# Layer normalisation of a graph-network pipeline moved between two engines, with the pipeline written out instead of looped

## The reference

```python
def _layernorm(x, axis=-1, eps=1e-05):
    m = jnp.mean(x, axis=axis, keepdims=True)
    v = jnp.var(x, axis=axis, keepdims=True)
    return (x - m) / jnp.sqrt(v + eps)

h = jnp.maximum(_layernorm(x, axis=-1), 0.0)
x = x + _L0_gnn_ref(h, adj, L0_gnn_W, L0_gnn_a)
h = jnp.maximum(_layernorm(x, axis=-1), 0.0)
x = x + _L1_gnn_ref(h, adj, L1_gnn_a0, L1_gnn_a1, L1_gnn_a2, L1_gnn_a3)
h = jnp.maximum(_layernorm(x, axis=-1), 0.0)
x = x + _L2_gnn_ref(h, L2_gnn_adj, adj, L2_gnn_weight, L2_gnn_bias)
h = jnp.maximum(_layernorm(x, axis=-1), 0.0)
x = x + _L3_gnn_ref(h, adj, L3_gnn_W, L3_gnn_a)
```

## Time and profile before

| | before |
|---|---|
| median of 3 runs | 351.57 us (351.4 to 351.6) |
| profiled execution, first to last instruction | 350.0 us |
| PE, DVE, ACT, POOL busy | 321.6, 312.2, 307.3, 252.4 us |
| instructions | 10115 |
| TensorE clock granted, mean | 0.993 |

### The profile page before, as it was taken

One profiled execution on the slowest core, in us unless ns is written; L12 is line 12 of the kernel. 1 busy time (PEld: TensorE's weight loads), 2 busy tenths in 40 slices (PEclk: granted clock), 3 DMA queues, 4 the chain that ended last, 5 costly groups with the idle time before them and its releaser, 6 DMA issues.

```text
span 350.0 us, 10115 instructions
## 1 busy us (share of the span) xinstructions
PE 321.6 (92%) x2568; PEld 293.3 (84%) x2568; DVE 312.2 (89%) x1603; ACT 307.3 (88%) x775; POOL 252.4 (72%) x396
## 2 busy tenths in 40 slices
PE   1899999999999997999999997999999999999981
PEld 0699899889989986979998986988998999988971
DVE  2889999989999969998999996998999999998864
ACT  1499889999999969999999986999999998999991
POOL 4866755898888644798988773589888875589632
PEclk9999999999999999999999999999999999999997
DMA  4900000550110000272101000057011000000011
GB/s 120 292 4 2 3 0 3 170 194 18 47 46 19 1 4 0 61 221 80 45 31 45 1 0 2 1 157 203 16 45 46 15 1 0 1 2 1 18 47 63
DMA packets 15976, 17.67 MB, mean 50 GB/s; under 512 B 2752, under 2 KB 11840, under 8 KB 15936
## 3 DMA queue, kind: packets, MB, share of 16 engines
q1 hardware_dynamic: 15936, 17.25, 16.3%
HBM read 13.05 MB, written 4.19 MB: 49 GB/s over the span
## 4 chain that ended last, share of the span: by engine, by line
PE 26%; issue 21%; POOL 21%; DVE 18%; ACT 9%; SPq 1%; DMA 1%; POOLq 1%; DVEq 0%; ACTq 0%
PE bank L844 6%; POOL rs L346 6%; POOL h L351 4%; DVE neg_s L595 4%; POOL xb L361 4%; PE bank L811 4%; ACT upper L450 3%; PE bank L778 3%; POOL h L354 3%; ACT prob L458 3%; PE bank L826 3%; DVE st L533 3%; POOL result L368 3%; PE bank L792 2%; PE bank L806 2%
## 5 line engine op out<-in xcount | busy, mean ns | idle before, releaser
L346 POOL TENSOR_TENSOR rs<-ve,minus_half 128x2 f32<-128x2 f32 x128 | 90.4, 706 | 62.6 <-DVE ve L552 61.5
L458 ACT ACTIVATE prob<-neg_s,neg_max 128x256 f32<-128x256 f32 x192 | 87.0, 502 | 10.9 <-DVE neg_max L595 10.4
L595 DVE CUSTOM_DVE_ANT_0 neg_s<-bank,upper 128x256 f32<-128x256 f32 x192 | 73.1, 416 | 9.2 <-ACT upper L450 6.9
L844 PE MATMUL bank<-val,pT 128*128 128x129 f32 x512 | 67.7, 275 | 0.0
L465 ACT ACTIVATE pT<-bank 128x512 f32<-128x512 f32 x96 | 57.7, 601 | 9.0 <-PE bank L826 8.0
L354 POOL TENSOR_TENSOR h<-h,rs 128x256 f32<-128x256 f32 x96 | 59.3, 617 | 7.5
L826 PE MATMUL bank<-ident,prob 128*128 128x128 f32 x384 | 58.0, 274 | 5.5 <-ACT prob L458 5.2
L844 PEld LDWEIGHTS bank<-val,pT 128*128 128x128 f32 x512 | 62.2, 191 | 0.2
L450 ACT ACTIVATE upper<-bank,val 128x256 f32<-128x256 f32 x128 | 52.6, 461 | 3.6 <-PE bank L815 3.4
L815 PE MATMUL bank<-absent,ident_bf 128*128 128x256 bf16 x192 | 52.8, 275 | 0.0
L811 PE MATMUL bank<-ident,val 128*128 128x128 f32 x256 | 47.2, 280 | 4.9 <-ACT val L441 3.6
(11 more groups left out here) (61 smaller groups left out, 656.2 us busy)
## 6 DMA issues: line engine op xcount, KB each, us to landing
edges<-in_adj SPq DMA_DIRECT2D x32, 256.0 KB, 3.0
xin<-in_x SPq DMA_DIRECT2D x32, 128.0 KB, 2.4
out_x<-result SPq DMA_DIRECT2D x32, 128.0 KB, 1.7
w_rel<-in_L_gnn_weight SPq DMA_DIRECT2D x1, 256.0 KB, 4.4
w_gat<-in_L_gnn_W SPq DMA_DIRECT2D x2, 64.0 KB, 2.0
a_gat<-in_L_gnn_a SPq DMA_DIRECT2D x4, 0.5 KB, 2.0
a_rel<-in_L_gnn_a SPq DMA_DIRECT2D x4, 0.5 KB, 3.5
bias<-in_L_gnn_bias SPq DMA_DIRECT2D x1, 64.0 KB, 4.7
```

The costliest lines, as they stand in the source:

```text
L346: pool.tensor_tensor(rs[:, k], ve[:, k], minus_half[:, :], ALU.pow).then_inc(rs_ready, 1)
L458: last = act.activation(prob[:, k % 4, t], neg_s[:, k % 4, t], ACT.Exp, bias=neg_max[:, k, t:t + 1], scale=-1.0)
L595: last = dve.tensor_tensor_reduce(out=neg_s[:, k % 4, t], in0=bank_z(k)[:, t], in1=upper[:, k % 4, t], scale=-1.0, scalar=3.0e38, op0=ALU. ...
L844: last = pe.matmul(bank_o(k)[:, t], pT[:, k % 4, u, t * P:(t + 1) * P], values[:, u], start=(u == 0), stop=(u == T - 1))
```

## The change

There are four edits.

1. The pipeline is written out. `pipeline(stages)` goes over all 128 units with constants; `eng.Fori` is gone, and so are the semaphore adds that stand beside SP's waits. The same stages run in the same order.
2. `center` goes from POOL to DVE. The two POOL operations of 128 x 256 become two DVE `tensor_scalar`, one a half of 128 x 128, which subtract the mean and multiply by the inverse deviation, both read from SBUF as a scalar for each partition. On DVE it stands at lag 1, for layers 0 and 3 behind `take_z`, for layer 1 just ahead of `rectify`. `less_mean` and its wait fall away.
3. `check_edges` is taken out on ACT. In its place the mask is computed as (adj - 1) * BIG on the adjacency read as unsigned, so that a value over 1 makes a score huge; the row maxima of layer 0 of all 32 graphs are kept (`neg_max0`), and at the end one comparison over 64 columns looks for such a value.
4. SP's load of the next adjacency waits for layer 0's mask and no longer for the check.

```diff
-    with eng.Fori(0, ROUNDS - 1) as rnd:
-        for s in range(PEELED, STEPS_A_ROUND):
-            step(s, rnd, rnd)
-        for s in range(PEELED):
-            step(s, rnd + 1, rnd)
+def pipeline(stages):
+    for s in range(len(ORDER) + LAG_MAX):
         for stage, lag, layers in stages:
+            if 0 <= s - lag < len(ORDER) and ORDER[s - lag][0] in layers:
+                stage(s - lag, *ORDER[s - lag])
...
-            def center(rnd, layer, k):
-                pool.wait_ge(rs_ready, nth(rnd, ALL, layer, k))
-                pool.tensor_tensor(h[:, k, :, 1:], (xin if layer == 0 else x1)[:, k],
-                                   mv[:, k, :, 0:1].to_broadcast([P, T, D]), ALU.subtract).then_inc(less_mean, 1)
-                pool.wait_ge(less_mean, nth(rnd, ATTEND, layer, k))
-                pool.tensor_tensor(h[:, k, :, 1:], h[:, k, :, 1:],
-                                   rs[:, k, :].rearrange("p (t o) -> p t o", o=1).to_broadcast([P, T, D]),
-                                   ALU.mult).then_inc(centered, 1)
...
-            def check_edges(rnd, layer, k):
-                act.wait_ge(edges_loaded[k], rnd * 16 + 16)
-                act.wait_ge(edges_checked, nth(rnd, RGCN_REL, 2, k))
-                act.activation(squares[:, :], edges[:, k].rearrange("p t n -> p (t n)"), ACT.Square,
-                               bias=minus_half[:, 0:1],
-                               accum_out=distances[:, bass.ds(rnd * SLOTS + k, 1)]).then_inc(edges_checked, 1)
...
+            def center(n, layer, g):
+                k = g % SLOTS
+                dve.wait_ge(rs_ready, nth(ALL, n))
+                for t in range(T):
+                    last = dve.tensor_scalar(h[:, k, t, 1:], (xin if layer == 0 else x1)[:, k, t],
+                                             mv[:, k, t, 0:1], rs[:, k, t:t + 1], ALU.subtract, ALU.mult)
+                last.then_inc(centered, 1)
...
-                                             edges[:, k, t].rearrange("p (q u) -> p u q", u=T),
-                                             0.0, -BIG, ALU.is_le, ALU.mult)
+                                             edges[:, k, t].bitcast(u32).rearrange("p (q u) -> p u q", u=T),
+                                             -1.0, BIG, ALU.add, ALU.mult)
...
-                           (invert_sums, 7, LAST), (mean_and_variance, 0, LAST), (residual, 7, FIRST),
+                           (center, 1, GATS), (invert_sums, 7, LAST), (mean_and_variance, 0, LAST), (residual, 7, FIRST),
...
-                           (residual, 7, MULTI_REL), (rectify, 1, MULTI_REL), (mean_and_variance, 0, FIRST)])
-            dve.wait_ge(edges_checked, B + 1)
-            dve.tensor_scalar(other[:, :], distances[:, :], T * N * 0.25 + 0.5, None, ALU.is_gt).then_inc(flag_step, 1)
+                           (residual, 7, MULTI_REL), (center, 1, MULTI_REL), (rectify, 1, MULTI_REL), (mean_and_variance, 0, FIRST)])
+            dve.wait_ge(z_taken, len(ORDER))
+            dve.tensor_scalar(other[:, :], neg_max0[:, :, :].rearrange("p b t -> p (b t)"), -0.5 * BIG, None,
+                              ALU.is_lt).then_inc(flag_step, 1)
```

More of the change, by code:

```diff
@@ L20, with nth @@
 ROUNDS = B // SLOTS
-STEPS_A_ROUND = 4 * SLOTS
 ALL, ATTEND, GATS, NORMED, MULTI_REL, RGCN_REL = (0, 1, 2, 3), (0, 1, 3), (0, 3), (1, 2), (1,), (2,)
 NOT_LAST, NOT_MULTI, FIRST, LAST = (0, 1, 2), (0, 2, 3), (0,), (3,)
+ORDER = [(layer, rnd * SLOTS + k) for rnd in range(ROUNDS) for layer in range(4) for k in range(SLOTS)]
+UNIT = {unit: n for n, unit in enumerate(ORDER)}
+COUNTS = {layers: list(itertools.accumulate(int(layer in layers) for layer, _ in ORDER))
+          for layers in (ALL, ATTEND, GATS, NORMED, MULTI_REL, RGCN_REL, NOT_LAST, NOT_MULTI, FIRST, LAST)}
 LAG_MAX = 9
[L27 to L48, removed]
-        for stage, lag, layers in stages:
[L50 to L53, removed]
-    for s in range(PEELED):
-        step(s, 0, None)
-    with eng.Fori(0, ROUNDS - 1) as rnd:
-        for s in range(PEELED, STEPS_A_ROUND):
-            step(s, rnd, rnd)
-        for s in range(PEELED):
-            step(s, rnd + 1, rnd)
[L62 to L65, removed]
+def nth(layers, n):
+    return COUNTS[layers][n]
+def pipeline(stages):
+    for s in range(len(ORDER) + LAG_MAX):
+        for stage, lag, layers in stages:
+            if 0 <= s - lag < len(ORDER) and ORDER[s - lag][0] in layers:
+                stage(s - lag, *ORDER[s - lag])
 GAT = ["stats", "aggr", "eps", "rstd", "norm", "xT", "hT", "wh", "v", "z", "relu", "e", "exp",
@@ L286, in store @@
[L286 to L291, removed]
-            for k in range(SLOTS):
[L295 to L307, removed]
@@ L426, in normalize, with take_hT @@
                 last.then_inc(h_ready, 1)
[L428 to L435, removed]
+            def take_hT(n, layer, g):
+                k = g % SLOTS
+                act.wait_ge(hT_put, nth(ATTEND, n))
+                act.activation(hT[:, n % 4], bank_x(n), ACT.Relu).then_inc(hT_ready, 1)
@@ L481, in _, with take_pT, elu_exponential @@
-            pipeline(act, [(take_v, 3, RGCN_REL), (elu_exponential, 8, LAST), (check_edges, 6, RGCN_REL),
+            def take_pT(n, layer, g):
+                k = g % SLOTS
+                act.wait_ge(pT_put, nth(ATTEND, n))
+                act.activation(pT[:, n % 4], bank_p(n), ACT.Copy).then_inc(pT_ready, 1)
+            def elu_exponential(n, layer, g):
+                k = g % SLOTS
+                act.wait_ge(o_taken, nth(ALL, n))
+                act.activation(expy[:, n % 4], y[:, n % 4], ACT.Exp).then_inc(expy_ready, 1)
@@ L639, in _, with elu @@
-            pipeline(dve, [(add_eps, 1, MULTI_REL), (elu_lower, 9, LAST), (statistics, 0, MULTI_REL),
+            def elu(n, layer, g):
+                k = g % SLOTS
+                dve.wait_ge(expm_ready, nth(LAST, UNIT[3, g]))
+                if g >= SLOTS:
+                    dve.wait_ge(stored[k], 16 * (g // SLOTS))
+                dve.tensor_tensor(result[:, k], expy[:, n % 4], y[:, n % 4], ALU.max).then_inc(elu_ready, 1)
+            pipeline([(add_eps, 1, MULTI_REL), (elu_lower, 9, LAST), (statistics, 0, MULTI_REL),
```

294 lines of the change are left out of this document (159 added, 135 removed).

## The result

The changed kernel takes 372.01 us (median, 371.44 to 372.28) against 351.49 for the kernel before on the same chip: the ratio is 1.0582, with a 95% interval of 1.0567 to 1.0597. It is 20.5 us slower. The forecast was 358 us with a range of 346 to 367, so the direction was right and the time is outside the range.

A forecast was written before the change was run, and what follows sets the result against it. PE, DVE and ACT were all near nine tenths busy; DVE and PE were the limits in octets 0 and 1. 350.0 - 5.1 (loop) + 12.2 (center) = 357.1 of span, plus 1.6 gives 358.7; forecast 358 us, range 346 to 367.

The forecast's parts named there:

- The loop: Pipeline written out: two DVE issue stalls at the loop's way back go, 2.76 less 0.21 us each, -5.1 us.
- The check and the loads: check_edges off ACT and earlier adjacency loads: worth nothing, since PE and DVE are as full and no row waits.
- DVE becomes the pace setter: With center on DVE, its round is 81.5 us against PE's 76, making DVE the most loaded engine.
- The price of a half: One 128-column center tensor_scalar on DVE costs 0.21 us in the queue, 0.42 a unit; outer bounds 0.137 and 0.30.
- Nothing waits for `center` on DVE: In DVE's queue center waits for its unit's power only at octet 3's start, some 0.1 us in two steps a round.
- Waits for POOL disappear: DVE's waits for POOL's center, 2.7 us a round in expy, mask and haT, vanish; nb's go on.
- Octet 3: Fourth eight-step stretch of a round: DVE replaces POOL as limit, 15.88 us becomes 16.7.
- The sum: A round of four octets is 23.9 + 23.6 + 19.6 + 16.7 = 83.8 us, +3.4; together +12.2 us.
- the dear one: Rival for center on DVE: a half costs 0.30 us, a round +6.4, time 370 us; chance 0.11.
- Free scalars: Rival for center on DVE: scalars cost nothing, 0.137 us a half, a round 79.6, time 344 us; chance 0.12.
- Relief counts: Rival: ACT and POOL relief counts, octets 22.9, 22.6, 19.0, 15.5, a round 80.0, time 345 us; chance 0.13.

The follow-up runs named there:

- experiment 2: The kernel before, only written out, with check_edges still on ACT, center on POOL and the 64-column comparison at the end; 345.78 us against 351.84.
- e1: The changed kernel with center back on POOL as two operations, all else as changed; 345.44 us against 351.84 for the kernel before.
- Experiment 6: The changed kernel with take_hT of layer 3 moved from DVE to ACT; 366.56 us, +15.3 over the kernel before. Its second run is e10.
- e5: The changed kernel with center's mean replaced by the constant 0.0, inverse deviation still read from SBUF; 362.93 us, +11.7 over the kernel before.
- experiment 5: The changed kernel with layer 1's center moved up DVE's list, ahead of the statistics' aggregation and away from rectify; 367.92 us, +16.1 over the kernel before.
- e3: The changed kernel with both scalars of center replaced by the constants 0.0 and 1.0; 354.66 us, +2.8 over the kernel before.
- e10: e1 (center on POOL) with take_hT of layer 3 moved from DVE to ACT; 347.60 us, -4.3 against the kernel before.
- e7: The changed kernel with center of layers 0 and 1 back on POOL, layer 3's on DVE; 354.21 us, +3.0 over the kernel before.
- e11: e1 with center of layer 1 alone on DVE, just ahead of rectify; 360.67 us, +8.3 over the kernel before.

## Why the prediction was wrong, step by step

Edit 2 was given +12.2 us and cost 26.9. Two steps of its sum failed: the price of a half was too low (0.21 us, measured 0.256), and `rectify`'s wait for `center` on DVE itself, about 4 us, was left out.

- *The loop (right).* -5.1 us was forecast, -6.1 measured in experiment 2. The next octet gave nothing back: 15.88 us before, 16.01 in e2. No wait of DVE for issue above 0.2 us is left in e1, e2 or the changed kernel, against the two of 2.8.
- *The check and the loads (right).* Nothing was given to them; 0.3 us measured.
- *DVE becomes the pace setter (right in direction).* Octet 0 came nearly as worked out by its own terms: 20.3 + 8 x 0.512 = 24.4 against 24.2. Experiment 6 shows that DVE is not alone.
- *The price of a half (wrong size; the largest step).* The bounds were 0.19 to 0.26, and I took 0.21, below even their middle of 0.225; it is 0.256. I had +0.05 from L582 and +0.06 from L616 for one scalar and treated the second as perhaps free, without any row that said so. Two of L616's would have been right. It makes 24 x 0.092 = 2.2 us a round on DVE. From 0.195 a half (e5, where the two halves of a unit put the next instruction 0.39 us behind their start) to 0.256 the time rose by 8.8 us, so the 0.046 are worth some 6.6 us, an estimate. At a price below the forecast's, e5 still takes 362.93 us and not 358: the price alone doesn't explain the miss.
- *Nothing waits for `center` on DVE (wrong; a term left out).* I looked at what `center` waits for, the power, and not at what waits for `center` on its own engine. `rectify` stands right behind it: 0.11 to 0.12 us a unit, about 4 us in experiment 5. In the kernel before it read what POOL had written long ago.
- *Waits for POOL disappear (right, with one left).* expy fell from a mean of 485 ns to 293 and mask from 315 to 282. One new collision a round appeared at the start of octet 1: the last `center` of layer 0 meets POOL's addition and takes 0.92 us instead of 0.59.

```profile
199.07 0.92 DVE L507 TENSOR_SCALAR h<-xin,mv,rs 128x128 f32<-128x128 f32 x2
```

```profile
198.93 0.72 POOL L326 TENSOR_TENSOR result<-result,x 128x256 f32<-128x256 f32 x1
```

- *Octet 3 (wrong size).* 16.7 forecast, 17.6 measured. The price of the halves explains about 0.4 of the 0.9: the octet grows by 0.48, from 17.16 to 17.64, between e5 and the changed kernel. The other half I can't place: with halves at 0.14 it still takes 16.68 us where 15.4 was worked out. The stall at `center` for the power was seen as forecast (0.1 us at 244.88, two steps a round).
- *The sum.* Forecast 83.8 a round, measured 87.2. The halves give 1.8 (2.2 us of DVE, of which the step from e5 returned four fifths), `rectify` 1.0, the collision 0.3: 3.1 of 3.4. That it nearly closes is partly luck. By the same method e3's price should give 79.6 and the run has 82.5, 2.9 more, of which `rectify` and the collision explain 1.3: the base of octets 1 and 3 was too low and DVE's added time was counted in full everywhere, and the two errors offset each other at the higher price. Round 0 was given 2.3 us, because DVE waits there for its first data, and grew by 5.6 over e1.
- *The rivals.* The time came out at the dear one (370), but not by its condition: it asked for 0.30 a half, and the half cost 0.256, by two scalars at 0.06 instead of a lost column rate; `rectify`'s wait, which no rival had, made up for it. Free scalars (344) would have been wrong even with free scalars: e3 is at 354.7. The table of the Trainium skill (VectorE: DVE Perf Modes, The TRN2 errata), by the estimate of 0.127 us without a term for scalars, fits e3's 0.14 and not the change's 0.256. *Relief counts* (345) wanted octets of 22.9, 22.6, 19.0 and 15.5; e3, with POOL and ACT relieved and DVE given the least that a `center` can cost, has 22.5, 23.6, 19.8 and 16.7. For ACT e1 against e2 says the same, 0.3 us.
- *The range* ended at 367 although the two ends of one term, 0.137 and 0.30, gave 344 and 370; both ends were outside it.

What stays open is what limits octet 3, where DVE's time is worth a little over half with `center` on DVE (e3, e5, e6) and nothing with it on POOL (e10). No run relieves POOL or PE alone.

## What to carry to other kernels

Price an operation that the trace doesn't have by its parts, and count each per-partition scalar on DVE as its own 0.06 us beside the columns until a row says otherwise; with halves of 128 columns the two scalars (0.12 us) cost nearly as much as the columns and the start together (0.14). When work moves onto a full engine, ask what reads its result on that same engine right behind it: that wait is new even if the operation is not. With three engines near nine tenths, both moves off the slack one lost here: to DVE 26.9 us, layer 3 to ACT 9.7. The gain was in the loop, and that edit alone beats both kernels (345.8 us, with the mask's check 345.4). Weigh such a move by stretch: the same microsecond of DVE counted nearly in full in two octets and a little over half in a third.

## What the runs showed of the hardware that was not expected

- POOL's `tensor_scalar` with two per-partition scalars takes 0.80 us for 128x128, more than its `tensor_tensor` for 128x256 (0.61).
- A two-column DVE operation can lose as much to POOL as a large one: `add_eps` lasts 0.15 us ahead of POOL's multiply of 128x256 and 0.58 us behind its start, in e7, e10 and e11. In e1 it started 0.01 us ahead of POOL and lost nothing.
- POOL's power does not hold DVE's masks up, but it seems that they can hold it up: behind `add_eps` at 197.52 the power took 1.21 us instead of 0.70, and two masks ran from 197.58 to 198.07, over its start. No run takes the two apart.

```profile
197.75 1.21 POOL L314 TENSOR_TENSOR rs<-ve,minus_half 128x2 f32<-128x2 f32 x1 [1.85 <-DVE ve L500]
```
